# Last graph layer: W1 applied to h before the edge sums, one accumulator held twice, scatter addresses computed in one run

## The reference, cut to what matters

```
h = maximum(layernorm(x), 0)                       # [6250, 32]
mi = zeros.at[dst].add(e * h[src])                 # sums over the edges into a node
mo = zeros.at[src].add(e * h[dst])                 # sums over the edges out of it
h4 = tanh(concat([mi, mo, h]) @ W1 + b1)           # W1: [96, 32]
... three more 32x32 layers with tanh ...          # x + result
```

## Time and profile before

| | us |
|---|---|
| median of 3 runs (lowest to highest) | 10885.63 (10884.3 to 10895.94) |
| the profiled execution | 10900.59 |
| its span in the trace | 10898.9 |
| granted TensorE clock, mean of the span | 0.689 of full speed |
| last layer's scatters, first to last start | 8649.0 to 10835.0 |

### The profile page before, as it was taken

One profiled execution on the slowest core, in us unless ns is written; L12 is line 12 of the kernel. 1 busy time (PEld: TensorE's weight loads), 2 busy tenths in 40 slices (PEclk: granted clock), 3 DMA queues, 4 the chain that ended last, 5 costly groups with the idle time before them and its releaser, 6 DMA issues. The chain is left out here.

```text
span 10898.9 us, 415021 instructions
## 1 busy us (share of the span) xinstructions
PE 8198.1 (75%) x156361; PEld 7430.5 (68%) x156362; DVE 7555.2 (69%) x18528; ACT 4639.3 (43%) x12099; POOL 5964.7 (55%) x5974
## 2 busy tenths in 40 slices
PE   6676767664773556655669977999999688888888
PEld 6676666664663555555568856777777488888886
DVE  5588888885773444454458847888888577777776
ACT  0011111111552333333346633544444477777775
POOL 0267777776335777777777716777777211111110
PEclk6555555555556777877789978999999655555555
DMA  1132233332003333333332212222222244444443
GB/s 43 5 87 76 73 76 75 74 75 56 12 9 92 112 112 112 109 111 110 114 105 79 79 26 66 63 61 63 63 62 63 63 115 117 115 115 116 116 116 82
DMA packets 850556, 875.92 MB, mean 80 GB/s; under 512 B 629005, under 2 KB 632517, under 8 KB 849966
## 3 DMA queue, kind: packets, MB, share of 16 engines
q1 hardware_dynamic: 622830, 526.55, 17.7%
q0 software_dynamic: 227648, 348.32, 12.5%
HBM read 631.25 MB, written 135.27 MB: 70 GB/s over the span
## 5 line engine op out<-in xcount | busy, mean ns | idle before, releaser
L1565 ACT ACTIVATE c_products<-c_pa 125x512 f32<-125x512 f32 x2368 | 1222.8, 602 | 1808.1 <-PE c_pa L1609 1795.2
L1440 POOL DMA_INDIRECT c_near_ranked<-h_rows,c_idx x1568 | 1678.6, 1071 | 477.9 <-issue 477.6
L778 POOL DMA_INDIRECT edges_by_rank<-rank_stage,rank_idx x1568 | 1603.3, 1023 | 503.6 <-issue 461.3
L1892 POOL DMA_INDIRECT edges_b<-c_send_rows,c_send_idx x1184 | 1317.8, 1113 | 399.2 <-issue 357.1
L1609 PE MATMUL c_pa<-c_near_apart,c_basis 32*125 32x128 f32 x18944 | 745.2, 294 | 1013.2 <-DVE c_near_apart L1528 911.5
L1609 PEld LDWEIGHTS c_pa<-c_near_apart,c_basis 32*125 32x125 f32 x18944 | 638.4, 195 | 1134.4 <-issue 1134.4
L2358 POOL DMA_DIRECT2D rows<-local_rows x548 | 298.0, 544 | 1990.4 <-DVE hot_d L2376 1820.0
L289 PE MATMUL acc_s<-hot_col,hot_row 128*123 128x91 f16 x3136 | 760.7, 410 | 696.4 <-ACT start_table L733 559.6
L2497 PE MATMUL acc_mi_mo<-msg,hot_e 128*128 128x32 bf16 x8768 | 1153.1, 205 | 152.3 <-issue 151.3
L1620 PE MATMUL c_py<-c_products,c_weights 125*64 125x128 f32 x18944 | 1226.0, 285 | 0.0
L289 PEld LDWEIGHTS acc_s<-hot_col,hot_row 128*123 128x123 f16 x3136 | 719.1, 320 | 730.9 <-issue 524.7
(11 more groups left out here) (404 smaller groups left out, 19928.7 us busy)
## 6 DMA issues: line engine op xcount, KB each, us to landing
rows<-local_rows POOLq DMA_DIRECT2D x548, 256.0 KB, 4.1
own_d<-hparts SPq DMA_DIRECT2D x2192, 48.0 KB, 2.9
hi_rows_in<-hi_rows SPq DMA_DIRECT2D x392, 256.0 KB
c_dst_rows_in<-dst_rows SPq DMA_DIRECT2D x148, 512.0 KB
near_by_rank<-c_near_ranked SPq DMA_DIRECT2D x98, 768.0 KB, 5.0
rows_both<-hi_rows SPq DMA_DIRECT2D x196, 196.0 KB
near_h<-c_near_h SPq DMA_DIRECT2D x74, 512.0 KB
c_near<-near_h SPq DMA_DIRECT2D x148, 256.0 KB
```

Of the source, the lines that this page charges most:

```text
L778: pool.indirect_dma_start(g.ranked, bass.IndirectOffsetOnAxis(idx[:, r, q:q + 1], 0), stage[:, r, q, :], None, bounds_check=last_rank, oob ...
L1440: pool.indirect_dma_start(near[:, b, q, :], None, g.h1_rows, bass.IndirectOffsetOnAxis(idx[:, b, q:q + 1], 0), bounds_check=last_node, oob ...
L1565: last = act.activation(by_round[:, half, r, rnd], pa[0:K3, r, 0:TR * P].rearrange("p (f e) -> p f e", f=width), ACT.Copy)
L1892: pool.indirect_dma_start(g.edges_b, bass.IndirectOffsetOnAxis(sending.idx[:, n, q:q + 1], 0), sending.rows[:, n, q, :], None, bounds_chec ...
```

## The change

h times a block of W1, summed over edges, equals the sum times that block. So `bucket_rows` first computes h times W1's first and second block (a transpose and four matmuls for each of 13 groups of node blocks, kept by ScalarE as `weighed`) and splits both products into bf16 parts. The gather then fetches rows that already carry W1, and both sides of an edge are added into the same 32 sums, so that mi and mo need no halves of their own. The room is used to hold each sum twice: `acc_upper_low` has 64 columns a block. One matmul that moves 64 columns adds the upper parts of `prod` (into the first copy) and of `rest` (into the second), and one of 32 columns adds `low` into the first: two matmuls a group where there were three. At the end VectorE adds the two copies, and the first dense layer has 64 inputs: the sums (an identity block as weights) and h.

The addresses of a quarter's 16 groups are asked for by `find_places` in one run before the scatters; the table load is moved into the middle of the gather. In set-up the row stores have four buffers and no wait after each one, W1 is loaded first, and the edge table uses the room of an older one. Line numbers after L244 move by 2 and more; L2483 becomes L2532, L116 L117.

```diff
-def bucket_rows(g, c):
+def bucket_rows(g, c, W1):
...
         @block.sync
         def _(sp):
+            for r in range(4):
+                for k in range(2):
+                    sp.dma_start(w_both[r * F:(r + 1) * F, k * F:(k + 1) * F], W1[k * F:(k + 1) * F, :]).then_inc(s_w1, 16)
+            sp.dma_start(g.edges[:, :, :], g.edges_b.rearrange("(p t) w -> p t w", p=P)).then_inc(s_edges, 16)
...
                 sp.wait_ge(s_tr16, m + 1)
-                sp.dma_start(g.local_rows[kind, q * P:q * P + n, :], rows16[0:n, m % 2, :]).then_inc(s_rows_out, 16)
-                sp.wait_ge(s_rows_out, (m + 1) * 16)
+                sp.dma_start(g.local_rows[kind, q * P:q * P + n, :],
+                             rows16[0:n, m % DEEP_R, :]).then_inc(s_rows_out[m % DEEP_R], 16)
...
-            split_parts(dve, st, [g.hparts[:, :, k, :] for k in range(3)], g.h[:, :, :], rest[:, :, :])
+            dve.wait_ge(s_weighed, 2)
+            for side in range(2):
+                split_parts(dve, st, [g.hparts[:, side, :, k, :] for k in range(3)],
+                            weighed[:, :, side * F:(side + 1) * F], rest[:, :, :])
...
+            for n in range(NG):
+                if n >= 2:
+                    pe.wait_ge(s_hT, n - 1)
+                pe.transpose(ph[:, n % 2, 0:P], g.h[:, 4 * n:4 * n + 4, :].rearrange("p b f -> p (b f)"),
+                             g.ident[:, :]).then_inc(s_hturn, 1)
+                if n:
+                    times_w1(n - 1)
...
+                def find_places(cols):
+                    for col in cols:
+                        for j in range(NJ):
+                            pe.compute_val((col * 2 + j * 2 * F) * 4 + PSUM_AT)
+
                 def add_up(half, h, cols):
                     for q in range(h * Q, (h + 1) * Q):
-                        for side, col in ((0, MI), (1, MO)):
+                        for side in range(2):
+                            at = slice(side * F, (side + 1) * F)
                             for j in range(NJ):
-                                for part in (upper(prod), upper(rest), low):
-                                    last = pe.matmul(acc[:, ds(cols[(q - h * Q) * 2 + side] + (col + j * F), F)],
-                                                     hot_e[:, half, q, side, j * P:(j + 1) * P],
-                                                     part[:, half, q, side * F:(side + 1) * F],
-                                                     start=False, stop=True, skip_group_check=True)
+                                both = acc[:, ds(cols[(q - h * Q) * 2 + side] * 2 + j * 2 * F, 2 * F)]
+                                hot = hot_e[:, half, q, side, j * P:(j + 1) * P]
+                                pe.matmul(both.rearrange("p (k f) -> p k f", k=2), hot, upper[:, :, half, q, at],
+                                          start=False, stop=True, skip_group_check=True)
+                                last = pe.matmul(both[:, 0:F], hot, low[:, half, q, at],
+                                                 start=False, stop=True, skip_group_check=True)
...
                     for h in range(2):
-                        gather(i, half, h, True)
+                        gather(i, half, h, True, 0)
                         cols = blocks_of(last, 1 - half, h)
+                        gather(i, half, h, True, 1)
+                        find_places(cols)
                         if h == 0:
                             pe.wait_ge(s_low, i * 2 + half)
                         add_up(1 - half, h, cols)
...
-                dve.memset(cat[:, NBS:NBLK, F:2 * F], 0.0)
-                dve.tensor_copy(cat[:, :, 0:F], acc[:, MI:MO].rearrange("p (b f) -> p b f", f=F))
-                dve.tensor_copy(cat[:, 0:NBS, F:2 * F], acc[:, MO:MO + NBS * F].rearrange("p (b f) -> p b f", f=F))
-                dve.tensor_copy(cat[:, :, 2 * F:3 * F], g.h[:, :, :]).then_inc(s_cat, 1)
-                dve.wait_ge(s_cat, 1)
+                st = Steps(dve, s_cat)
+                st.add(dve.tensor_copy(ws[0][0:F, :], g.ident[0:F, 0:F]))
+                st.add(dve.tensor_copy(cat[:, :, F:2 * F], g.h[:, :, :]))
+                st.do(dve.tensor_copy(cat[:, :, 0:F], parts[:, :, 0, :]))
+                st.do(dve.tensor_tensor(cat[:, :, 0:F], cat[:, :, 0:F], parts[:, :, 1, :], ALU.add))
```

More of the change, by code:

```diff
@@ L66 @@
 FAR = 6.5e7
+PSUM_AT = 1 << 25
 ROWS, COLS = HI + NA, 64 + ND1
@@ L2259, in _, with times_w1 @@
                 act.wait_ge(s_tr, m + 1)
-                if m >= 2:
-                    act.wait_ge(s_rows_out, (m - 1) * 16)
-                act.activation(rows16[0:n, m % 2, :], ptr[0:n, m % 2, 0:P], ACT.Copy).then_inc(s_tr16, 1)
+                if m >= DEEP_R:
+                    act.wait_ge(s_rows_out[m % DEEP_R], m // DEEP_R * 16)
+                act.activation(rows16[0:n, m % DEEP_R, :], ptr[0:n, m % 2, 0:P], ACT.Copy).then_inc(s_tr16, 1)
         @block.tensor
         def _(pe):
+            def times_w1(n):
+                pe.wait_ge(s_hT, n + 1)
+                if n == PER:
+                    pe.wait_ge(s_weighed, 1)
+                for r in range(4):
+                    at = slice(r * F, (r + 1) * F)
+                    last = pe.matmul(pw[:, r, n % PER * 2 * F:(n % PER + 1) * 2 * F], hT[at, n, :], w_both[at, :],
+                                     start=True, stop=True)
+                last.then_inc(s_mul, 1)
+            pe.wait_ge(s_w1, 8 * 16)
+            for n in range(NG):
+                if n >= 2:
[4 more added lines that the diff above has]
+                    times_w1(n - 1)
+            times_w1(NG - 1)
             pe.wait_ge(s_edges, 16)
@@ L2394, in split_rest @@
                     dve.wait_ge(s_read, i * 4 + (half * 2 + 2))
-                    dve.tensor_tensor(rest[:, half, :, :], prod[:, half, :, :], upper(prod)[:, half, :, :],
+                    dve.tensor_tensor(rest[:, half, :, :], prod[:, half, :, :], upper[:, 0, half, :, :],
                                       ALU.subtract).then_inc(s_rest, 1)
@@ L2399, in split_low @@
                     dve.wait_ge(s_rest, i * 2 + (half + 1))
-                    dve.tensor_tensor(low[:, half, :, :], rest[:, half, :, :], upper(rest)[:, half, :, :],
+                    dve.tensor_tensor(low[:, half, :, :], rest[:, half, :, :], upper[:, 1, half, :, :],
                                       ALU.subtract).then_inc(s_low, 1)
@@ L2473, in ready, with gather @@
                     pe.wait_ge(s_own_d[half], i * (SH * 16) + SH * 16)
-                def gather(i, half, h, waits):
-                    if waits:
+                def gather(i, half, h, waits, part):
+                    if waits and part == 0:
                         pe.wait_ge(s_read, i * 4 + (half * 2 + h))
-                    for q in range(h * Q, (h + 1) * Q):
+                    for q in range(h * Q + part * Q // 2, h * Q + (part + 1) * Q // 2):
                         for side, hot, own in ((0, hot_s, own_s), (1, hot_d, own_d)):
@@ L2485, in gather @@
                                                  start=(n == 0), stop=(n == NJ * 3 - 1))
-                    last.then_inc(s_gat, 1)
+                    if part:
+                        last.then_inc(s_gat, 1)
                 def blocks_of(i, half, h):
@@ L2515, in _ @@
                 for h in range(2):
-                    gather(0, 0, h, h > 0)
+                    for part in range(2):
+                        gather(0, 0, h, h > 0, part)
                 chunk(0, 1, 0)
@@ L2573, in turn @@
                 for b in range(4):
-                    last = pe.transpose(pt[0:3 * F, n % 2, b * P:(b + 1) * P], cat[:, n * 4 + b, :], g.ident[:, :])
+                    last = pe.transpose(pt[0:2 * F, n % 2, b * P:(b + 1) * P], cat[:, n * 4 + b, :], g.ident[:, :])
                 last.then_inc(s_tr, 1)
```

66 lines of the change are left out of this document (46 added, 20 removed).

## The result

The median of four runs is 10521.96 us (10519.82 to 10529.68) against 10886.36 (four runs, 10884.3 to 10895.94): a ratio of 0.9665, 95% interval 0.9648 to 0.9682. That is 364 us less where 260 were forecast, 103 us faster than the predicted 10625. The profiled execution took 10529.68 for a span of 10527.7 us.

A forecast was written before the change was run, and what follows sets the result against it. TensorE's own instruction sequencer was taken to bound the last layer. Gains of 219 (quarters), 12 (clock) and 29 us (set-up) sum to 260, taking the 10885.6 median to 10625; own range 10560 to 10690, wider range 10470 to 10720.

The forecast's parts named there:

- The quarter: Last layer, 16 groups' gather and scatter: 3.59 us instead of 3.99, over 548 quarters 219 us less.
- The lead of 17 matmuls: TensorE's sequencer in the last layer: about 17 matmuls queued ahead, covering 0.43 us of a stop in the gather.
- The clock: Last layer: less idle makes stretches granted 1.00 likelier, counted as 12 us of gain.
- rival A: Last layer: array or other engines bound it, through 2.4 GHz or a deeper queue; 10370 to 10540 us, chance 0.17.
- a granted clock above 0.7: Last layer: together with quarters of 3.1 us, named as a sign that the prediction was wrong.
- Moving it hides no more than before: Table load moved to mid-gather: still stalls 0.34 us, 0.35 with the restart, against 0.42 before.
- Register instructions out of the scatter: this is the gain: Last layer's scatter: 16 groups take 1.28 us instead of 2.02, and the full lead covers most bookkeeping between quarters.
- The merge alone gives the array nothing: Scatter groups: two matmuls take 53 + 27 = 80 ns, what the three took.
- Set-up: Ahead of the last layer: faster row stores, less the new work, gain 29 us, between 20 and 33.
- Its floor of 3.1 a quarter: ScalarE in the last layer: its chunk work takes 3.1 us a quarter, below the forecast 3.59.
- B: Last layer: costlier register instructions or 64-column matmuls add 0.2 to 0.4 a quarter; 10735 to the old time, chance 0.14.
- C: Last layer: run of register instructions not covered at all, quarter 4.68 us, 11235 us; chance 0.05 including other losses.

The follow-up runs named there:

- e6: Changed kernel with the table load back behind the whole gather, the run of eight register instructions right behind it: 10800.4 us, ratio 0.9913.
- e4: Changed kernel with the run of eight register instructions cut in two, four behind the gather and four in mid-scatter: 10412.9 us, ratio 0.9555.
- e8: Changed kernel with 12 of a quarter's 48 gather matmuls done twice, ahead of the run of register instructions: 10665.5 us, ratio 0.9783.
- e1: Changed kernel with the set-up's 36 row stores again on two buffers and each waited for: 10577.83 us, ratio 0.971.
- e12: e4 with three 32-column matmuls a group instead of the merged two: 10415.4 us, ratio 0.9567.
- e2: Changed kernel with three 32-column matmuls a group again, run of register instructions and moved load kept: 10664.3 us, ratio 0.9783.
- e7: Changed kernel with three matmuls a group and the address in front of each group, leaving the moved load and new set-up: 10628.9 us, ratio 0.9751.
- e10: Changed kernel with three matmuls a group and the load behind the gather, the run right behind it: 10911.6 us, ratio 1.0006.
- e3: Changed kernel without the run, each group's address computed in front of its two matmuls: 10621.3 us, ratio 0.9748.
- e9: Changed kernel with the load behind the gather and no run, keeping the merged matmuls and new set-up: 10892.1 us, ratio 0.9990.
- e11: e4 with two of ScalarE's eight block copies a chunk left out, so sums differ: 10416.5 us, ratio 0.9553.

## Why the prediction came out as it did, point by point

**The quarter.** At the granted clock 0.50, the state it was computed for, it is 3.564 us; forecast 3.59. Term by term, averages over such quarters: load stop 0.34 (0.369 from start to start less 0.027; forecast 0.35), run stop 0.62 (0.65), scatter 1.246 plus one start, 1.27 (1.28), end of quarter 0.07 less 0.027, 0.04 (0.03). The eight register instructions start 0.133 us apart, and 0.078 + 0.057 had been assumed. 548 such quarters would save 233 us; forecast 219.

**The lead of 17 matmuls.** The sequencer reached the load at 9321.5, by when 7 of 24 gather matmuls had started: 17 were queued again, and e6 and e4 changed the stops by what that lead says. The Trainium skill (TensorE: Matmul & The Clock Gate, table at the top) gives TensorE's queue a depth of 64. By that, as an estimate, no stop would exceed 0.2 us; the trace disagrees in every quarter, as the run's stop was never under 0.60.

**The clock: the mis-sized term.** Forecast 12 us. The layer took 1853.7 instead of 548 x 3.564 = 1953: 99 us. The direction ("less idle makes such stretches likelier") was right and e8 shows it, but I had read the single warm stretch of before as rare and took rival A's third of the time for a side case; half of the quarters lay wholly at 1.00, and another eighth in part. One of the prediction's signs of being wrong, a granted clock above 0.7, so came true (0.76 in the layer), though the quarters went only to 3.38 and not to 3.1. e1, with the same stream, had 0.75. The Trainium skill (TensorE: Matmul & The Clock Gate, "What's actually happening") says that activity releases the throttle. In e8, e4 and e12, where TensorE does more in the same time, the trace agrees (0.88, 0.91, 0.98). It is no full order: e6 with its quarter of 3.86 us had 0.70 and e2 with 3.61 had 0.63. What sets the share there stays open.

**"Moving it hides no more than before": this step failed.** It is true of the load's own stop (0.34 against 0.42) and false of the kernel. Before, the load emptied the queue right ahead of the scatter, and the register instructions, 0.124 us apart, then paced it from its first group. With the load in mid-gather the scatter begins with a full queue and lasts 1.63 instead of 1.97 us. That alone is worth 240 us (e7), 72% of the layer's gain, and 244 to 260 in the three pairs of the table. The sum did count it without naming it: the 0.43 us taken off the run of eight is the queue that refills behind the moved load.

**"Register instructions out of the scatter: this is the gain": this failed too as an attribution.** The run by itself costs 35 us (e10), or 30 once the load is moved (e2 against e7), as it is a stop of 0.62 in one piece. At 1.2 GHz it gains nothing even with the merge. Of e3's few quarters at 0.50 hardly any close a turn, so the four places in a turn are averaged one by one: 3.58 us in e3, 3.57 in the changed kernel. It pays at 2.4 GHz, where e3 stays near 3.5, bound by its sequencer, and the changed kernel falls to 3.229. The prediction put both moves into one sum from one starting point, so that its total held and its parts did not. My reading of the old group as three matmuls of 0.080 plus a register instruction of 0.046 gave 0.126 by chance: with two matmuls between them the instructions are still 0.124 apart.

**"The merge alone gives the array nothing": right** (e9, and e3 against e7: 6 us). It gives 123 us beside the run and the moved load (e2), by the groups of 0.0555 us instead of 0.075 at 1.00 and because more of the layer is granted 1.00 (0.76 against 0.63 in the mean), and next to nothing again once other engines bound the quarter (e12: 17 us of the layer, the intervals of the ratios overlap).

**Set-up.** Forecast 29, measured 24.3. The stores took 18.8 us (forecast 16), and e1 gave 33.4 back; but they began 9.3 us later behind the mark than before (44.3 against 35.0), where 6 were allowed. The thirteen turns of h take 1.04 us each, not the 0.6 estimated from transpose and copy: the estimate left out the four matmuls. From start to start the transpose takes 0.40 and the matmuls 0.64, back to back on TensorE, and the copy lies beside them.

**The other engines.** ScalarE's wait for TensorE fell from 460 us to 108, lower than half because the warm quarters go below what was forecast. Its floor of 3.1 a quarter is where e4 ended, although not by ScalarE alone (e11).

**Of the rivals,** A's half came true: not the queue, but a clock mean of 0.76 in the layer; its figure of 10540, for a third of the time at 2.4 GHz, was the nearest of all. B and C did not occur: the 64-column matmul and the register instruction cost what the nearest rows gave.

## What to carry to other kernels

When one engine's own sequencer is late, list its stops (table loads, register arithmetic, branches) and ask for each what is queued in front of it and what it leaves for the next; two stops back to back share one cover, and a short stop that stands apart costs little (here 0.13 us of 0.53), so cut a long run before hoisting it. Test the parts of such a change alone, since a right total can hide that one moved line carries most of it. And a stretch at 0.5 of the clock is not a constant of the kernel: when a change makes TensorE denser, work out both levels for each quarter.

## What was not expected of the hardware

- Register instructions on TensorE's sequencer come 0.124 us apart whether two or three matmuls with their weight loads lie between them (e3, e7, before), and 0.133 apart with nothing between them when they have six operations (74 ns each) instead of the shorter 46 ns.
- In a pair of a 64- and a 32-column matmul at 1.2 GHz the second starts 0.027 us after the first, and the next pair 0.053 after that; I had expected the 0.053 first. The sum is the 0.080 computed. At 2.4 GHz both distances are 0.028.
- The stage before the last layer ended anywhere between 8522 and 8549 us in executions of identical instructions. Spans of single executions are to be compared from a mark behind such a stage.
